# A decoder block's last phase: PSUM pairs dealt out anew, the next batch's attention rows one MLP tile earlier

## What is computed

```
x = x + attention(norm(x))          # causal, 16 heads of 16, rope; then @ Wout + bout
x = x + xattn(norm(x), ctx, ctx)    # see below
x = x + ffn(norm(x))                # ternary weights, 1024 wide, exact gelu

# xattn(Q, K, V): LN1 of all three, 16 heads of 64
q, k = l2norm(Q1 @ wq), l2norm(K1 @ wk);  out = q (k^T v)       # no softmax
y = Q + out @ wo + bo
y = y + gelu(LN2(y) @ w1 + b1) @ w2 + b2                        # 1024 wide
```

## Time and profile before

| | |
|---|---|
| median of 3 runs | 1338.8 us (1336.12 to 1340.1) |
| profiled execution, its own time | 1340.68 us |
| its span, first to last instruction | 1338.7 us |
| mean granted clock of TensorE | 0.898 of full speed |
| busy: PE / DVE / ACT / POOL | 1062.5 / 798.1 / 660.4 / 423.2 us |
| the last phase | from about 680 us to the end |
| one full round | 81.8 us, six of them |

### The profile page before, as it was taken

One profiled execution on the slowest core, in us unless ns is written; L12 is line 12 of the kernel. 1 busy time (PEld: TensorE's weight loads), 2 busy tenths in 40 slices (PEclk: granted clock), 3 DMA queues, 4 the chain that ended last, 5 costly groups with the idle time before them and its releaser, 6 DMA issues. The chain is left out here.

```text
span 1338.7 us, 23286 instructions
## 1 busy us (share of the span) xinstructions
PE 1062.5 (79%) x7133; PEld 781.2 (58%) x7133; DVE 798.1 (60%) x1705; ACT 660.4 (49%) x1166; POOL 423.2 (32%) x556
## 2 busy tenths in 40 slices
PE   3777058788999984884478899898989989899886
PEld 2444023343444442773367788777878777788775
DVE  4888356576777762763446646656565565654643
ACT  1334115565666674562137355473654637447443
POOL 0344226566333331110344232332313333132301
PEclk9677558899999996897689899898999989999997
DMA  2332423333222204166411121101211012010000
GB/s 86 106 114 75 126 88 113 113 105 113 94 91 88 74 34 136 64 247 245 135 47 64 48 79 47 60 18 47 78 47 63 16 47 78 0 63 17 1 17 16
DMA packets 52989, 103.82 MB, mean 78 GB/s; under 512 B 6656, under 2 KB 32768, under 8 KB 48832
## 3 DMA queue, kind: packets, MB, share of 16 engines
q1 hardware_dynamic: 49756, 95.62, 21.0%
q0 software_dynamic: 1920, 6.03, 1.4%
q10 hardware_dynamic: 1252, 1.39, 0.3%
HBM read 63.05 MB, written 39.58 MB: 77 GB/s over the span
## 5 line engine op out<-in xcount | busy, mean ns | idle before, releaser
L802 ACT ACTIVATE p_probs<-p_psS 128x512 f32<-128x512 f32 (+1 forms) x352 | 181.2, 564 | 125.5 <-ACTq L801 122.9
L704 DVE CUSTOM_DVE_ANT_0 p_psA<-p_psA,p_mask 128x512 f32<-128x512 f32 (+1 forms) x256 | 155.7, 647 | 106.4 <-DVEq L702 106.0
L836 PE MATMUL p_psA<-p_ks,p_qs 96*128 96x512 bf16 (+3 forms) x512 | 145.1, 319 | 36.8 <-PEq L834 36.5
L855 PE MATMUL p_psS<-p_qs,p_ks 99*128 99x256 bf16 (+3 forms) x512 | 132.3, 312 | 21.7 <-PEq L880 12.5
L1658 ACT ACTIVATE p_h<-p_psG,w_columns 128x512 f32<-128x512 f32 x128 | 88.2, 689 | 121.6 <-ACTq L1657 121.0
L1995 PE MATMUL p_psY<-p_n,p_hh 128*128 128x256 f32 x512 | 117.2, 313 | 35.8 <-PEq L1986 29.7
L1773 DVE TENSOR_TENSOR p_hl<-p_h,p_hh 128x512 fp32r<-128x512 f32 x128 | 86.7, 687 | 88.9 <-DVEq L1772 86.6
L723 POOL TENSOR_SCALAR_AFFINE_SELECT p_probs<-p_probs 128x512 f32<-128x512 f32 x128 | 80.6, 634 | 134.1 <-POOLq L722 114.7
L1995 PEld LDWEIGHTS p_psY<-p_n,p_hh 128*128 128x128 f32 x512 | 95.6, 218 | 41.8 <-issue 41.3
L866 PE MATMUL p_psO<-p_probs,p_v 128*32 128x512 f32 (+3 forms) x1024 | 93.1, 458 | 26.4 <-PEq L862 25.1
L1571 POOL TENSOR_TENSOR p_var<-p_mv,p_eps 128x4 f32<-128x4 f32 x24 | 8.1, 338 | 334.0 <-POOLq L1577 201.8
(11 more groups left out here) (251 smaller groups left out, 2824.2 us busy)
## 6 DMA issues: line engine op xcount, KB each, us to landing
p_n<-n_parts SPq DMA_DIRECT2D x16, 1024.0 KB, 6.7
o_sums<-p_o SPq DMA_DIRECT2D x32, 256.0 KB, 2.7
n_parts<-p_nh SPq DMA_DIRECT2D x8, 1024.0 KB, 3.9
n_parts<-p_nl SPq DMA_DIRECT2D x8, 1024.0 KB, 6.0
q_parts<-p_part SPq DMA_DIRECT2D x48, 128.0 KB
p_qs<-q_parts SPq DMA_DIRECT2D x32, 192.0 KB
p_x<-in_x_dram SPq DMA_DIRECT2D x8, 512.0 KB, 4.4
p_qs<-q_parts SPq DMA_DIRECT2D x32, 128.0 KB
```

Of the source, the lines that this page charges most:

```text
L704: nc.vector.tensor_tensor_reduce(out=bank[:, 0:w], in0=bank[:, 0:w], in1=mask[:, S - w:S], scale=1.0, scalar=MASKED, op0=ALU.add, op1=ALU.max,
L802: nc.scalar.activation(probs[:, g % 2, at:at + n * w], psS[place(s, turn) % SB][:, 0:n * w], ACT.Exp, scale=SCALE).then_inc(exp_done, 1)
L836: last = nc.tensor.matmul(bank[:, z * w:(z + 1) * w], qs[0:SROWS, k, g * G + r0 + z, i * P:(i + 1) * P], ks[0:SROWS, k, g, 0:w], start=Tru ...
L855: last = nc.tensor.matmul(bank[:, z * w:(z + 1) * w], key, qs[0:SROWS + MROWS, k, h, j * P:S], start=True, stop=True)
```

## The change

It sets four things. The pairs: M and T get pair 0; sums, attention rows and X get pair 1. The fixed tiles of the next batch: norms at M0, attention rows at M1, their addition at M2, moments at M3, `z1` at M5, so each one tile earlier. The transposes of the next batch: first half behind M5's finish and second half behind M7's, instead of behind M6's and X0's. Their readers: ScalarE reads the first half behind M7 and the second behind X1 (before: behind X0 and X2), VectorE subtracts the first behind M7's split and the second at the end of X2 (before: at the end of X2, and at X3 behind `scaled`). Nothing is added or taken away: every instruction is there as often as before.

```
@@ -1406,12 +1406,15 @@
         LAG = 3
         SQ = 6
         Q, M, X, T = "query", "mlp", "cross", "ternary"
-        M_PAIR, A_PAIR, X_PAIR, T_PAIR = 0, 1, 0, 1
+
+
+        M_PAIR, T_PAIR = 0, 0
+        S_PAIR, A_PAIR, X_PAIR = 1, 1, 1
         Z2_AT = (3, 5)
         Z3_AT, Z3_READ = (4, 6), (6, 7)
-        Z1_AT, Z1_READ = (M, 6, X, 0), (0, 2)
+        Z1_AT, Z1_READ = (M, 5, M, 7), 1
         Z1_FIRST, Z1_FIRST_READ = (3, 5), (5, 7)
-        NORMS_AT, ROWS_AT, ADD_AT, MOMENTS_AT, Z1_MADE = 1, 2, 3, 4, 6
+        NORMS_AT, ROWS_AT, ADD_AT, MOMENTS_AT, Z1_MADE = 0, 1, 2, 3, 5
         TB = P // 32
         POOL_FROM = 3
 
@@ -1455,7 +1458,7 @@
         psG = [ps(f"psG{i}", [P, S]) for i in range(LAG)]
         psY = [ps(f"psY{i}", [P, S]) for i in range(4)]
         psT = ps("psT", [P, S])
-        sums = psY[2 * T_PAIR]
+        sums = psY[2 * S_PAIR]
 
         const_in = sem("const_in")
         bias_in = sem("bias_in")
@@ -1691,13 +1694,16 @@
                         gelu(w["b1"], u, m)
                         if front and m == NORMS_AT:
                             norms()
+                        if more and m == XT - 1:
+                            affine(fh, w["ln1_g"], w["ln1_b"], 0)
                     elif kind == X:
                         act.wait_ge(qn_ready, 1)
                         act.sem_inc(qn_ready, -1)
                         nc.scalar.activation(hh[:, s, :], h[:, s, :], ACT.Copy).then_inc(qh_dve if m < POOL_FROM else qh_pool, 1)
-                        read = Z1_READ if back else Z1_FIRST_READ
-                        if more and m in read:
-                            affine(fh, w["ln1_g"], w["ln1_b"], read.index(m))
+                        if back and more and m == Z1_READ:
+                            affine(fh, w["ln1_g"], w["ln1_b"], 1)
+                        if not back and m in Z1_FIRST_READ:
+                            affine(fh, w["ln1_g"], w["ln1_b"], Z1_FIRST_READ.index(m))
                         if back and m in Z3_READ:
                             plain(Z3_READ.index(m))
                     else:
@@ -1775,7 +1781,7 @@
             def inverse_norms():
                 dve.wait_ge(norm_ready, 1)
                 dve.sem_inc(norm_ready, -1)
-                nc.vector.engine_nop().then_inc(pair_free[T_PAIR], 1)
+                nc.vector.engine_nop().then_inc(pair_free[S_PAIR], 1)
                 stepped(nc.vector.tensor_scalar(n2[:, :], n2[:, :], 1e-12, None, ALU.max))
                 stepped(nc.vector.reciprocal(n2[:, :], n2[:, :]))
                 stepped(nc.vector.tensor_copy(rh[:, :], n2[:, :]))
@@ -1880,6 +1886,8 @@
                             aggregate(mv1, var1_ready)
                         if more and m == Z1_MADE:
                             z1()
+                        if more and m == XT - 1:
+                            affine_low(fl, fh, 0)
                         if not front and m == XT - 1:
                             add_mlp(old)
                             stepped(moments(x2))
@@ -1906,10 +1914,8 @@
                                 scaled_low((u - 1) % LAG)
                             scaled_low(s)
                             if back and more:
-                                affine_low(fl, fh, 0)
+                                affine_low(fl, fh, 1)
                         if back and m == 3:
-                            if more:
-                                affine_low(fl, fh, 1)
                             dve.wait_ge(rs3_ready, 1)
                             dve.sem_inc(rs3_ready, -1)
                             norm3((0, 1), False)
@@ -2027,8 +2033,8 @@
 
             def head_sums(j):
                 if j == 0:
-                    pe.wait_ge(pair_free[T_PAIR], 1)
-                    pe.sem_inc(pair_free[T_PAIR], -1)
+                    pe.wait_ge(pair_free[S_PAIR], 1)
+                    pe.sem_inc(pair_free[S_PAIR], -1)
                 for t in range(4 * j, 4 * j + 4):
                     for b in range(TB):
                         last = nc.tensor.matmul(sums[32 * b:32 * b + 32, 0:P], select[:, t, :], sq[:, t % SQ, b * P:(b + 1) * P],
```

## The result

| | before | changed |
|---|---|---|
| median (9 runs each) | 1338.8 us | 1329.67 us |
| range of the runs | 1336.05 to 1343.97 | 1326.62 to 1335.37 |
| ratio, 95% interval | | 0.9933 (0.9915 to 0.995) |
| span of the profiled execution | 1338.7 us | 1324.7 us |
| mean granted clock | 0.898 | 0.913 |

The forecast was 1339.1; the time came within 2 us of rival B (1331.3), and the bound of 1335 for "same" was passed. The spans of the two profiled executions differ by 14.0 us, more than the medians. About 4 us of that is there before the first full round, where the change moves no work (that round's first sums stand at 720.96 us before and at 716.83 after). (The last phase starts earlier than the 680 us given above: its first query product on TensorE stands at 662.43 us before.)

The account below looks back on a forecast made before the run. TensorE was taken to bound the kernel, with only idle and half-clock time to win. Six rounds' -9.4, clock falls' +7.8 and the last two-half round's +1.9 gave +0.3 us: 1339.1, range 1329 to 1346.

Parts of the forecast that it names:

- rival B: Full rounds: the clock stays up in most, so the kernel is faster, -7.5 us to 1331.3; chance 0.27.
- same: Whole kernel: outcome not told from no change, within about 0.3% or 4 us; chance 0.44.
- The banks: Bank pairs: new pairs cost no waits, and the 3.65 us gap before X0's product loses its last releaser.
- First MLP, +1.15: First MLP of a full round: norms ahead of M1's split make M1's product 1.15 us later.
- Entry into X, -1.56: From X to the ternary stage: it starts 1.56 us earlier per full round at full clock, the 1.15 included.
- the last round's 12.57 us: End of X: time from `scaled` X3 to the first ternary matmul without next-batch transposes, used to price full rounds.
- Last round with both halves, +1.9: Last round with back and front halves: ScalarE waits for the sums, so M1's product comes 1.9 us later.
- The clock, +7.8: X in six full rounds: clock falls at X2's product for 6.9 us, +1.3 a round, +7.8 in all.
- ends of 0 and 2.1: X in full rounds: a clock fall costs 0 before X0's product, 2.1 us behind X2's product.

Follow-up runs that it names:

- e2: The changed kernel with the old bank pairs put back, so only the tile and transpose moves remain: 1330.02 us, ratio 0.9931.
- e3: The changed kernel with the next batch's norms put back from M0 to M1: 1323.38 us, ratio 0.9889.
- e6: The changed kernel with norms back at M1 and VectorE's first-half `affine_low` moved to X2: 1318.34 us, ratio 0.9854.
- e5: The changed kernel with VectorE's first-half `affine_low` moved from behind M7's split to X2, ahead of X2's split: 1325.18 us, ratio 0.9893.
- e1: The kernel before with the new bank pairs alone, all tiles and transposes left in place: 1336.4 us, ratio 1.0.
- e4: The kernel before with eight matmuls nobody reads put inside the 3.65 us gap ahead of X0's product: 1332.27 us, ratio 0.9955.
- e10: e7 with TensorE's `z_split` wait moved from X2 to X3 and six unread matmuls ahead of X3's product: 1322.09 us, ratio 0.9885.
- e8: e3 with the old bank pairs put back: 1323.05 us, ratio 0.9877.
- e7: e6 with VectorE's order at X2 and X3 changed, X2's split ahead of the moments: 1328.39 us, ratio 0.9934.
- e11: e6 with six unread matmuls put ahead of X2's product: 1315.06 us, ratio 0.9821.
- e9: e1 with eight unread matmuls put ahead of X2's product: 1328.39 us, ratio 0.9923.

## Why the prediction was wrong

By its steps:

- **The banks.** Right that the 3.65 us gap went and that VectorE came next. But the new pairs brought no time: the same tiles with the old pairs are as fast (e2).
- **First MLP, +1.15.** Right in kind, a little too large: the bracket has 0.81 us of idleness, by starts M1's product is 0.97 us late (it starts at 971.85; the issue ahead of it began at 969.50 and takes 1.38, so 970.88 was possible), and taking it away won 1.0 us a round (e3). TensorE followed the split by 0.15 us there, not 0.30.
- **Entry into X, -1.56.** Right: 1.83 measured, at full clock, which is 1.56, the 0.2 by which M1's product was less late, and 0.1 of small errors. That the last round's 12.57 us could stand for the end of X held to 0.01 us.
- **Last round with both halves, +1.9.** Right: M1's product waits 1.61 us, and from the second sums (1204.71) to the first ternary matmul (1246.92) it takes 42.21 us against 40.36. The six rounds' 10.8 less this 1.85 is 8.9; the medians differ by 9.1.
- **The clock, +7.8.** This is the step that failed: "I take it to fall in each full round, at the product of X2". It fell in none of the six. With the term left out the sum is the rival's 1331.3. The price for such a fall was itself about right (1.3 was said, with ends of 0 and 2.1; 1.33 in e6, 1.6 in e5, 1.8 in e1); it was charged for something that did not happen. The gap before X2's product, behind which the fall was put, was forecast at 2.3 us and came out at 1.71. No run has a gap of 2.3 there in the changed kernel; at 2.10 us the clock fell in two of six rounds (e5) and in five of six (e6). The prediction had one row for a fall behind 2.46 us of idleness and one for none behind 2.65, called both open, and chose by likeness to the middle round, whose gap of 3.65 us was much longer than any left.

The reading of the gap also had a flaw that the sum hid. The trace of before says in the bracket 3.65 us for the pair, and I had written that TensorE could win idle time and half-clock time. Of the idle time nothing was to be had (e4: the wait stays, the whole 1.85 us is won). The half clock counts there because the second transposes, and through them ScalarE's reads, `affine_low` and the normalisations on VectorE, stood behind it. This is what the moved tiles undid; the pairs were not needed for it.

The Trainium skill's rule that was weighed (TensorE: Matmul & The Clock Gate, section Why this matters for your kernels: long idle gaps between bursts drop the clock) came out right for the changed kernel, whose gaps of 1.07, 1.71 and 1.50 us left it up. It is not safe below 3 us: gaps of 2.10 (e6) and 2.82 us (e1) were followed by a fall in some rounds of one kernel and not in others.

What stays open: what sets the rounds in which the clock falls apart from those in which it does not, behind the same gap, and which of them get the long fall.

## What to carry to other kernels

When a wait is the longest on the bound engine, ask what stands behind it before asking what it costs: here the wait itself was free and only the half clock over the transposes behind it was paid for. When a change has two parts, try each alone: here one brought all and the other nothing. And look at what the fix puts in elsewhere (the norms ahead of M1 cost 1.0 us a round). Where a gap of 2 to 4 us cannot be closed, matmuls that nobody reads, in front of a product that waits anyway, can be worth as much as moving work (e4 and the change: 80.0 us a round both). They are no guarantee: e10 had them and its clock fell in two rounds.

## What the runs showed of the hardware that I had not expected

The same gap in the same code can be followed by a fall of the clock in one round and not in the next: in e1 a round of 79.98 us at 1.00, then rounds of 81.8 at 0.96. Counted over the six full rounds of each profiled execution:

| kernel | longest gap of TensorE in X, us | rounds with a fall in or behind it |
|---|---|---|
| before | 3.65 | 6 of 6 |
| e1 | 2.82 | 5 of 6 |
| e2 / e8 | 2.73 | 6 of 6 / 5 of 6 |
| e5 / e6 | 2.10 | 2 of 6 / 5 of 6 |
| e7 | 1.95, and 1.03 right behind | 6 of 6 |
| e10 | 1.81 | 2 of 6 |
| changed / e3 | 1.71 | none |
| e11 / e4 / e9 | 1.50 / 1.30 / 1.30 | none |

(e4's one fall lies behind M0, as told above.) When it falls, the half clock lasts about 6.8 us (each full round of the kernel before, two of e6) or 3.4 us (three of e6). And added TensorE work shortened three kernels: e4 by 6.2 us against the kernel before (ratio 0.9955), e9 by 8.0 against e1, e11 by 3.3 against e6.
